# Attention scores of 16-wide heads: a six-slot bf16 split against a three-slot float32r split with two heads side by side on TensorE's row halves

## The reference

```
h  = ln(x);  q, k, v = split(h @ W_attn + b)           # block 0: causal self-attention
x  = x + attn(q, k, v) @ W_aproj                       #   scores * 1/4, causal mask, softmax
x  = x + attn(ln(x) @ Wq, ctx @ Wk, ctx @ Wv) @ Wcproj #   cross-attention, 120 keys
x  = x + gelu(ln(x) @ W_fc) @ W_mproj
...                                                    # block 1: the same shape, relu, norms behind
scores = where(mask != 0, float32.min, scores)         #   its self-attention has a 256x256 mask
...                                                    # block 2: cross-attention with a mask per element
...                                                    # block 3: cross-attention, heads of width 64
```

## Time and profile before

| what | value |
|---|---|
| span of the profiled execution | 4385.8 us (2.4 us under the median of the timed runs, which is the only other time of an execution) |
| TensorE busy (PE) | 4260.8 us, 97% |
| TensorE weight loads (PEld) | 3436.5 us, 78% |
| VectorE busy (DVE) | 3663.2 us, 84% |
| ScalarE, GpSimd | 58%, 36% |
| mean granted TensorE clock | 0.989 |
| pass `l0`, `l1`, `l2` | roughly the first, second and third of three equal parts |

### The profile page before, as it was taken

One profiled execution on the slowest core, in us unless ns is written; L12 is line 12 of the kernel. 1 busy time (PEld: TensorE's weight loads), 2 busy tenths in 40 slices (PEclk: granted clock), 3 DMA queues, 4 the chain that ended last, 5 costly groups with the idle time before them and its releaser, 6 DMA issues. The chain is left out here.

```text
span 4385.8 us, 99261 instructions
## 1 busy us (share of the span) xinstructions
PE 4260.8 (97%) x33536; PEld 3436.5 (78%) x33536; DVE 3663.2 (84%) x12709; ACT 2547.7 (58%) x6753; POOL 1590.0 (36%) x2709
## 2 busy tenths in 40 slices
PE   5999999999999899999999999999999999999998
PEld 3788888888887677777777777778888888888886
DVE  4899999999997899999999999967777777777774
ACT  2556656566565545455454554536676767676765
POOL 3445454454452234444444444431222222222222
PEclk8999999999999999999999999999999999999999
DMA  5555455554553544545444454433222222222220
GB/s 172 147 154 161 133 151 153 140 161 138 149 157 114 152 132 137 141 127 163 133 146 132 133 149 124 135 98 84 62 78 61 79 61 79 61 77 63 72 66 9
DMA packets 406443, 513.40 MB, mean 117 GB/s; under 512 B 133808, under 2 KB 373936, under 8 KB 384432
## 3 DMA queue, kind: packets, MB, share of 16 engines
q1 hardware_dynamic: 398544, 496.82, 39.7%
q10 hardware_dynamic: 7392, 10.24, 0.7%
HBM read 266.30 MB, written 236.72 MB: 115 GB/s over the span
## 5 line engine op out<-in xcount | busy, mean ns | idle before, releaser
L816 ACT ACTIVATE probs_own<-bank 128x384 f32<-128x384 f32 (+2 forms) x1280 | 644.6, 569 | 80.0 <-DVE bank L1065 41.7
L723 ACT ACTIVATE ht<-bank,columns_l 128x256 f32<-128x256 f32 x384 | 197.2, 569 | 729.4 <-PE bank L1242 726.3
L625 POOL TENSOR_SCALAR veps<-meanvar 128x2 f32<-128x2 f32 x256 | 63.9, 249 | 1357.1 <-DVE meanvar L966 1357.1
L1189 PE MATMUL bank<-ht,w_ff 128*128 128x256 f32 x2048 | 489.8, 382 | 2.7 <-ACT ht L723 1.6
L1189 PE MATMUL bank<-w_ff,ffh 128*128 128x256 f32 x2048 | 475.7, 380 | 0.0
L1046 DVE DVE_READ_ACCUMULATOR2_ANT nmf_own<- 128x1 f32 x3072 | 433.5, 141 | 0.0
L1189 PEld LDWEIGHTS bank<-w_ff,ffh 128*128 128x128 f32 x2048 | 378.7, 190 | 49.4 <-issue 1.2
L1046 DVE CUSTOM_DVE_ANT_0 bank<-bank,mask_rows 128x256 f32<-128x256 f32 x1024 | 398.8, 457 | 21.2 <-PE bank L1189 21.1
L1189 PEld LDWEIGHTS bank<-ht,w_ff 128*128 128x128 f32 x2048 | 369.6, 190 | 50.0 <-ACT ht L723 2.8
L1189 PE MATMUL bank<-kstack_own,qstack_own 96*128 96x256 bf16 (+2 forms) x3072 | 370.1, 248 | 27.2 <-DMA kstack_own<-k_parts 18.7
L881 ACT ACTIVATE probs_other<-bank,negmax 128x120 f32<-128x120 f32 x1024 | 356.6, 383 | 59.6 <-DVE negmax L1169 59.6
(11 more groups left out here) (164 smaller groups left out, 10138.4 us busy)
## 6 DMA issues: line engine op xcount, KB each, us to landing
qstack_own<-q_parts SPq DMA_DIRECT2D x96, 768.0 KB, 5.7
kstack_own<-k_parts SPq DMA_DIRECT2D x64, 768.0 KB, 7.3
qstack_other<-q_parts SPq DMA_DIRECT2D x64, 768.0 KB, 5.9
q_parts<-q_parts_own SPq DMA_DIRECT2D x96, 384.0 KB, 2.5
q_parts<-q_parts_own SPq DMA_DIRECT2D x96, 256.0 KB, 2.3
k_parts<-k_parts_own SPq DMA_DIRECT2D x64, 384.0 KB, 2.9
q_parts<-other_parts SPq DMA_DIRECT2D x64, 384.0 KB, 2.5
other_words<-k_parts SPq DMA_DIRECT2D x64, 360.0 KB, 3.3
```

Source lines behind the costliest of these rows:

```text
L625: nc.gpsimd.tensor_scalar(veps[key][:, :], meanvar[key][:, :, 1], r["norms"][key]["eps"], None, ALU.add).then_inc(veps_ready.sem, 1)
L723: return nc.scalar.activation(out, in_, ACT.Identity, scale=scale, bias=bias)
L816: nc.scalar.activation(probs[key][0:rows, j % a.slots, 0:n], bank_of(u)[0:rows, 0:n], ACT.Exp, scale=a.scale).then_inc(a_done.sem, 1)
L1189: return nc.tensor.matmul(out, lhsT, rhs, start=first, stop=True, skip_group_check=True)
```

## The change

**Two parts in place of three.** q and k are split into a float32r part (`split_hi`, ACT writes it rounded) and the rest, also float32r (`split_lo`, now a DVE step that reads PSUM and writes the part itself). `split_rest`, `split_mid` and GpSimd's `split_lo` are gone, with their buffer `remains`. Three slots (`Q_SLOTS` (0, 0, 1), `K_SLOTS` (0, 1, 0)) of 16 rows give 48 rows; the parts have 4 bytes where they had 2, so the stacks have the same bytes.

**Two heads on row halves.** Even heads have their stack on partitions 0 to 47, odd heads on 64 to 111. `scores_max` and `scores_exp` jobs now go in pairs: one step of the list issues the matmuls of two jobs, alternating between rows 0 to 63 and rows 64 to 127 of the array, into two banks that it has both taken first. The second job of the pair issues nothing. The maxima have two parts (`negate` has two steps and `negate_t` turns them in float32), and `scores_exp` has 50 rows. `stack_q`, `stack_k` and `nm_rows` are two DMAs each, one per row half.

**Masks.** The causal mask of `l0`'s `scores_max` is added on TensorE by a matmul of `identb` with `causal_rows` behind each job's scores (full array, bf16), and DVE uses one `tensor_reduce` per job. In `l1` half of the `scores_exp` jobs get their mask in the same way (`mask_less`, 512 columns), and `mask_scores` on DVE does the other half. `l1`'s and `l2`'s `scores_max` masks stay on DVE.

**Order.** `LISTS`, `START` and `SPREAD` are all new. The last step of an element of `l2` is listed 5.41 periods behind its start (3.97 before). A copy of block 3's `w_q` to DRAM scratch is added to the first loads on SyncE's queue, and block 3's `ot3` shares `ffh`.

```diff
-PARTS = 3
-Q_SLOTS = (0, 0, 0, 1, 2, 1)
-K_SLOTS = (2, 1, 0, 0, 0, 1)
+PARTS = 2
+HF = H // FT
+Q_SLOTS = (0, 0, 1)
+K_SLOTS = (0, 1, 0)
...
-START = {"l0": 0.0, "l1": 33.12879, "l2": 66.18842}
+START = {"l0": 0.00000, "l1": 32.78467, "l2": 65.64606}
...
+def tile_rows(f, n):
+    return slice(f * P // FT, f * P // FT + n)
...
-                runs = r["scratch"][x, key].rearrange("n (d h) t -> (n d) h t", d=D)
+                runs = r["scratch"][x, key].rearrange("n (d h) (f t) -> f (n d) h t", d=D, f=FT)
...
+                for f in range(FT):
+                    sp.dma_start(stack[tile_rows(f, KS), :, :], runs[f]).then_inc(stacked[x, key].sem, 16)
...
             elif kind == "scores_max":
+                if j % 2:
+                    continue
...
-                bank = take(u)
-                for n, h in enumerate(heads):
-                    ins = mm(bank[:, n * nk:(n + 1) * nk], qstack[key][0:KS, stack_place(h), t * P:(t + 1) * P],
-                             r["kstack"][key][0:KS, stack_place(h), 0:nk], n == 0)
+                two = [take(u), take(plan["PE"][n_u + 1])]
+                for i in range(n):
+                    for f in range(FT):
+                        at = heads[i] // FT
+                        ins = mm(two[f][:, i * nk:(i + 1) * nk], qstack[key][tile_rows(f, KS), at, t * P:(t + 1) * P].bitcast(F32R),
+                                 r["kstack"][key][tile_rows(f, KS), at, 0:nk].bitcast(F32R), i == 0)
...
+                for bank in two if a.max_on == "pe" else ():
+                    whole = bank[:, 0:n * nk].rearrange("p (h k) -> p h k", k=nk)
                     if a.masked == "causal":
                         ins = mm(whole[:, :, nk - P:nk], identb[:, :],
                                  causal_rows[:, None, P:T].broadcast_to((P, n, P)), False)
...
             elif kind == "scores_exp":
+                if j % 2:
+                    continue
...
+                else:
+                    for t in range(QT):
+                        for f in range(FT):
+                            ins = part(f, j // FT, two[f][:, t * T:(t + 1) * T], slice(t * P, (t + 1) * P), slice(0, T), t == 0)
...
-                v.tensor_copy(nm_t[key][:, :], bank_of(u)[0:PARTS * H, 0:T // 2].bitcast(BF16)).then_inc(d_done.sem, 1)
+                v.tensor_copy(nm_t[key][:, :].bitcast(F32R), bank_of(u)[0:PARTS * H, 0:T]).then_inc(d_done.sem, 1)
...
     r["atts"] = {"own": Att("causal", (w_own[:, 0], bq0, "0"), (w_own[:, 1], bk0, "0"), (w_own[:, 2], None, "0"), w_own[:, 3], bv0, "causal",
-                            "dve", "pool"),
+                            "pe", "pool"),
...
     own = Att("self", (w_own[:, 0], col["q_b"], "0"), (w_own[:, 1], col["k_b"], "0"), (w_own[:, 2], None, "0"), w_own[:, 3], spr["v_b"], "all",
-              "dve", "dve")
+              "dve", "half")
```

More of the change, by code:

```diff
@@ L10 @@
 BF16 = mybir.dt.bfloat16
+F32R = mybir.dt.float32r
 U8 = mybir.dt.uint8
@@ L617, in _ @@
             kind, key, j = u.tag
-            if not blank and kind != "stats":
+            if not blank and u is not plan["POOL"][0]:
                 blank = True
@@ L1339, in _ @@
                     pe.wait_ge(nm_rows[key].sem, w.value(nm_rows[key], ("nm_rows", key, 0)))
-                if a.on_pe(j) and a.masked == "each":
+                if (a.on_pe(j) or a.on_pe(j + 1)) and a.masked == "each":
                     if w.new(d_done, ("mask", "m", 0)):
                         pe.wait_ge(d_done.sem, w.value(d_done, ("mask", "m", 0)))
-                bank = take(u)
-                heads = a.exp_heads(j)
-                at, kq = stack_place(heads[0]), slice(0, KS + PARTS)
+                two = [take(u), take(plan["PE"][n_u + 1])]
@@ L1346, in _, with part @@
                 ks, qs = r["kstack"][key], qstack[key]
+                def part(f, at, out, keys, queries, first):
+                    kq = tile_rows(f, KS + PARTS)
+                    return mm(out, ks[kq, at, keys].bitcast(F32R), qs[kq, at, queries].bitcast(F32R), first)
                 if a.cross:
[L1348 to L1350 removed]
+                    for n in range(2):
+                        for f in range(FT):
+                            ins = part(f, a.exp_heads(j)[n] // FT, two[f][0:S2, n * T:(n + 1) * T], slice(0, S2), slice(0, T), n == 0)
+                            if n and not a.on_pe(j + f):
+                                ins.then_inc(a_full.sem, 1)
+                elif a.kind == "causal":
+                    for f in range(FT):
+                        part(f, j // FT, two[f][:, 0:T], slice(0, P), slice(0, T), True)
+                    for f in range(FT):
+                        ins = part(f, j // FT, two[f][:, T:T + P], slice(P, T), slice(P, T), False)
+                        if not a.on_pe(j + f):
+                            ins.then_inc(a_full.sem, 1)
+                else:
+                    for t in range(QT):
+                        for f in range(FT):
+                            ins = part(f, j // FT, two[f][:, t * T:(t + 1) * T], slice(t * P, (t + 1) * P), slice(0, T), t == 0)
+                            if t and not a.on_pe(j + f):
+                                ins.then_inc(a_full.sem, 1)
@@ L1351, in _ @@
+                for f in range(FT):
+                    bank = two[f]
+                    if not a.on_pe(j + f):
+                        continue
+                    if a.cross:
                         ins = mm(bank[0:S2, :].rearrange("p (h t) -> p h t", h=2), identb[0:S2, 0:S2],
                                  m_cols[:, None, :].broadcast_to((S2, 2, T)), False)
-                elif a.kind == "causal":
-                    mm(bank[:, 0:T], ks[kq, at, 0:P], qs[kq, at, :], True)
-                    ins = mm(bank[:, T:T + P], ks[kq, at, P:T], qs[kq, at, P:T], False)
-                    if a.on_pe(j):
+                    elif a.kind == "causal":
```

500 lines of the change are left out of this document (229 added, 271 removed), and 6 rows, old and new, of the table SPREAD.

## The result

The changed kernel takes 4964.05 us (median of four runs, 4963.69 to 4972.02), the kernel before on the same chip 4390.12 us: a ratio of 1.131 [1.129, 1.133], 574 us slower. The forecast was 4588 us, with a range up to 4765. The direction was right; the size was missed by 376 us.

The account below looks back on a forecast made before the run. The prediction took TensorE's instruction stream to bound all three passes. Its terms, -363 + 113 + 17 + 271 + 162 = +200 us with the rest at 0, added to 4388 gave 4588 us, range 4420 to 4765.

Parts of the forecast that it names:

- Step 1: Score matmuls on TensorE: pairs on row halves run together at the bf16 pace, halving the score stream, -363 us.
- step 5: Weight loads left uncovered behind changes of shape on TensorE: +162 us, with 0.05 us taken per float32r load.
- Step 2: Causal masks of l0's scores_max and half of l1's scores_exp moved to TensorE: +113 us.
- Step 3: Turning the maxima in float32 on TensorE, 320 turns at 0.110 us in place of 0.056: +17 us.
- Step 4: Changes between row halves and other array shapes on TensorE: 3,013 more at 0.09 us each, +271 us.
- rival (d): float32r weights load as slowly as f32, so loads bound short pairs: 4764 us; chance 0.10.
- Step 6: DVE, ACT and GpSimd savings hidden by TensorE's stream, DMAs with the same bytes and no steady waits: 0, up to -30 us.
- Step 7: Order and banks: pairs waiting for two banks, longer l2 chain, added copy delaying first stacks: 0, at most +40 us.
- (c): The order loses more: 1,728 pairs wait 0.05 us each for a second bank, 86 us, about 4675; chance 0.10.
- DVE at 75%: Sign in the changed kernel's profile: DVE's busy share down to some 75%.
- the 0.09 and 0.10 around a run: Sign: the row ahead of a row-half run 0.09 us longer, a full-array f32 group behind one 0.10 longer.
- TensorE busy for 97% or more: Sign: TensorE still 97% busy or more; idle over 5% in mid-pass would make the reasoning wrong.

Follow-up runs that it names:

- e5: The changed kernel with stacks reading back mostly one head in eight, and the parts of q, k and the maxima in bf16: 4538.22 us, 1.035 of before.
- e2: The changed kernel with every stack but each pass's first element's reading back only one head in eight: 4719.98 us, 1.075 of before.
- e6: e2 with each two pairs of scores_exp directly behind one another on TensorE, 3,346 changes of shape instead of 3,652: 4728.45 us, 1.078 of before.
- e7: e2 with the masks on TensorE left out and added nowhere else: 4642.57 us, 1.058 of before.
- micro_dma: DMAs alone, no kernel work: q and k together take 8.2 us as one DMA per tile, 12.5 as two over 48 partitions each in 1 KB pieces.

## Why the prediction came out wrong

The 574 us come apart by runs: 4387 to 4538 (e5) is what the change does without float32r operands and without waits for stacks, **151 us**; 4538 to 4720 (e2) is the float32r operands, most of it their loads, **182**; 4720 to 4964 (the changed kernel) is the reading of the full stacks, **244**. The sum is 577; the 3 us are those between the medians of before on two chips.

**Step 1** (half of the score stream, -363) held in kind. Row halves run together, and one record is enough. A float32r matmul of 256 columns takes 0.120 in a long run of singles ((3.64 - 2.68) / 8), not 0.110, and pairs have the same pace ((3.07 - 2.59) / 4): 23 us over 2,304 pairs. For short pairs see step 5.

**Step 2** (masks, +113) held in the kernel before: 111 in steady work. **Step 3** (turns, +17) was not tested by itself.

**Step 4** (changes of shape, 0.09 each, +271) was right: 0.107 with bf16 on both sides, and 0.15 with the load in e6's `l0`. With the load's bf16 bound in step 5, the prediction's own sum is 4388 + 200 - 54 = 4534, and e5 measured 4538. That the sum fits doesn't prove each term, since errors may cancel; e7's open remainder is a reason for care.

**Step 5** failed in its size. "I take the turns' 0.05, one record of 4-byte data" was a guess between two rows of one step; the load turned out at 193 ns, and rival (d) had it. It had a chance of 0.10, which was too little: the nearest rows in kind, 4-byte weights that are not turned, were the float32 loads of 190 ns in the earlier trace rows. Against bf16 loads (d) comes to 54 + 176 = 230 us; e5 measured 182, of which some 23 are step 1's streaming. Why the loads cost less than (d) has it was not tested; that the last short pair of a run has no next load to wait for is one possible reason. Of the 182 us, 128 were not in the forecast: about 105 of loads and 23 of streaming.

The Trainium skill's page "TensorE: Matmul & The Clock Gate", section "Weight-path perf modes — Fast Weight Load (FWL) and DoubleRow", says that fast weight load is on for 128 weights of a type other than FP32, and that it brings FP32 nothing. Read so that float32r counts as FP32, the trace agrees (193 against 94 ns).

**Step 6** failed in its last sentence, and with it the largest piece: "The DMAs carry the same bytes, and no steady stretch waits for them." The bytes did stay (515.67 MB in all, 513.40 before), and in the kernel before steady work did not wait for the stacks. But the same bytes in two DMAs over half the partitions each, in 1 KB pieces, take 12.5 us instead of 8.2 (micro_dma), and the kernel before had 10.2 us between issue and first use. Two numbers that stood in the trace, the landing of the second stack (7.3 us, issued 1.15 us after the first) and the 10.2 us, leave a slack of 1.8 us, less than the 4.3 that split and pieces cost. Step 7 set only the queue's first stacks and the order at risk, and the rivals had a mechanism for lost order (c), at 86 us, but none for the DMAs. The miss of 376 us is these 244, the 128 of the float32r operands and 4 of all else.

Of the signs that the prediction named: DVE at 75% came, 0.111 for short pairs came as rival (d), the 0.09 and 0.10 around a run came. TensorE busy for 97% or more did not: it was 94%. Its idle time in mid-pass reached 4.0% in `l0` and 4.5% in `l1`, and 5.3% in `l1` from 2000 to 2400 us, past the 5% that was to make the reasoning wrong.

## What to carry to other kernels

Packing matmuls side by side pays by the length of an unbroken run, not by the count of matmuls. Here a run on row halves costs about 0.38 us for its two changes of shape with their loads and saves 0.06 per matmul of 256 columns against singles of the same type, so it breaks even between six and seven; count the runs in the order before the stream.

When a change leaves a DMA's bytes alone but alters its partitions or pieces, set its new duration against the distance from its issue to its first use. If that slack is smaller than the growth, the wait comes once per element, and here the clock's dip behind it added about half as much again.

## What the runs showed of the hardware that was not expected

A float32r weight load is as slow as a float32 one even with 48 rows (193 ns), and in a run of short matmuls it sets the pace: 0.111 us for 120 columns, in pairs ((2.96 - 2.51) / 4) as in singles ((3.51 - 2.62) / 8). Two DMAs of 384 KB into 48 partitions each take 6.7 us where one of 768 KB into 96 takes 5.1.
